# A mixture-of-experts layer split by choice: first choices placed and computed first, second choices scattered beside the first expert tiles, results in a ring of 18 tiles

## What is computed

```python
def _L0_ffn_ref(x, router_w, w1, w2, w3):
    logits = flat @ router_w.T
    topk_probs, topk_idx = jax.lax.top_k(softmax(logits), 2)
    topk_probs = topk_probs / (sum(topk_probs) + 1e-09)
    h = silu(flat @ w1[e].T) * (flat @ w3[e].T)      # for the chosen experts e; 341 wide
    out = sum over the two choices of gate * (h @ w2[e].T)
```

## Time and profile before

| what | us |
|---|---|
| median of 3 timed runs | 1537.77 (1532.89 to 1538.66) |
| the profiled execution, its own time | 1534.53 |
| its span, first to last instruction | 1532.7 |
| busy: PE / DVE / ACT / POOL | 1106.3 / 916.4 / 650.8 / 571.1 |

### The profile page before, as it was taken

The page is one execution under the profiler, slowest core; times in us unless marked ns, Lnnn a source line. Parts: engine busy times, 40 slices in busy tenths (PEclk is TensorE's granted clock), DMA queues, the critical chain, the costliest instruction groups (busy, mean ns, idle before and its releaser), DMA issues.

```text
span 1532.7 us, 23197 instructions
## 1 busy us (share of the span) xinstructions
PE 1106.3 (72%) x6172; PEld 880.5 (57%) x6172; DVE 916.4 (60%) x3422; ACT 650.8 (42%) x1813; POOL 571.1 (37%) x575
## 2 busy tenths in 40 slices
PE   3454578128784039999999946759999499999970
PEld 3444466115563028888888723335554299999970
DVE  5555578865887015555555569686763255555545
ACT  3777747203442002222222247726775144444430
POOL 2000000000677744444444400005777455555553
PEclk9999999999985569999999979968999699999995
DMA  9991000000111112222222370001121122222228
GB/s 236 428 430 83 2 1 1 0 0 1 41 53 53 52 45 60 58 62 61 59 61 60 117 246 15 0 0 36 53 67 51 47 74 70 70 72 69 70 59 308
DMA packets 60177, 125.43 MB, mean 82 GB/s; under 512 B 13148, under 2 KB 40676, under 8 KB 58512
## 3 DMA queue, kind: packets, MB, share of 16 engines
q0 software_dynamic: 20000, 73.21, 12.8%
q1 hardware_dynamic: 40048, 50.76, 11.7%
HBM read 50.75 MB, written 74.99 MB: 82 GB/s over the span
## 4 chain that ended last, share of the span: by engine, by line
PE 56%; DVE 19%; ACT 8%; issue 7%; POOL 6%; DMA 3%; SPq 1%; DVEq 0%; POOLq 0%; ACTq 0%
PE bank L1288 15%; PE bank L1279 8%; PE bank L1276 6%; PE bank L1277 6%; POOL rows L869 6%; PE bank L366 3%; PE bank L181 2%; PE bank L1465 2%; PE bank L1472 2%; PE bank L1264 2%; PE bank L1439 2%; DMA u<-planes 2%; ACT work L1379 1%; PE bank L1400 1%; ACT u L215 1%
## 5 line engine op out<-in xcount | busy, mean ns | idle before, releaser
L1150 POOL DMA_INDIRECT planes<-pay,goal x284 | 294.9, 1038 | 305.4 <-DVE pay L1197 251.0
L869 POOL DMA_INDIRECT rows<-pay,slot x256 | 251.9, 984 | 383.1 <-issue 346.7
L1288 PE MATMUL bank<-pay 128*128 128x128 f32 (+1 forms) x1988 | 275.1, 278 | 0.5 <-DVE pay L1216 0.2
L1288 PEld LDWEIGHTS bank<-pay 128*128 128x128 f32 (+1 forms) x1988 | 255.2, 191 | 26.6 <-DVE pay L1216 16.5
L1244 ACT ACTIVATE pay<-bank 128x256 f32<-128x256 f32 (+1 forms) x213 | 81.4, 382 | 309.4 <-PE bank L1277 275.3
L1248 ACT ACTIVATE pay<-bank,pay 128x256 f32<-128x256 f32 x284 | 125.8, 474 | 163.7 <-PE bank L1279 163.6
L1216 DVE TENSOR_TENSOR pay<-pay,bank 128x256 f32<-128x256 f32 (+1 forms) x213 | 82.7, 415 | 129.2 <-ACT pay L1244 128.7
L1170 DVE COPY pay<-wreg 128x1066 f32 (+1 forms) x142 | 100.0, 704 | 71.5 <-issue 66.4
L1279 PE MATMUL bank<-pay 128*128 128x256 f32 x568 | 135.9, 383 | 0.6 <-DVE pay L1180 0.6
L1276 PE MATMUL bank<-pay 128*128 128x256 f32 (+1 forms) x426 | 127.9, 382 | 0.6 <-DVE pay L1180 0.6
L1277 PE MATMUL bank<-pay 128*128 128x256 f32 (+1 forms) x426 | 127.2, 380 | 0.0
(11 more groups left out here) (387 smaller groups left out, 1984.4 us busy)
## 6 DMA issues: line engine op xcount, KB each, us to landing
rows<-pay POOLq DMA_DIRECT2D x10, 3432.0 KB, 55.6
pay<-rows SPq DMA_DIRECT2D x142, 130.0 KB
u<-planes SPq DMA_DIRECT2D x64, 256.0 KB, 5.9
planes<-pay,goal POOLq DMA_INDIRECT x284, 2.3
wreg<-in_w SPq DMA_DIRECT2D x1, 4264.0 KB, 24.9
wreg<-in_w SPq DMA_DIRECT2D x1, 4120.0 KB, 13.0
X<-in_x SPq DMA_DIRECT2D x2, 2048.0 KB, 20.1
rows<-pay,slot POOLq DMA_INDIRECT x256, 2.3
```

Of the source, the lines that this page charges most:

```text
L869: self.nc.gpsimd.indirect_dma_start(out=xs, out_offset=bass.IndirectOffsetOnAxis(ap=self.t["slot"][:, k, q:q + 1], axis=0), in_=self.t["pa ...
L1150: nc.gpsimd.indirect_dma_start(out=planes, out_offset=bass.IndirectOffsetOnAxis(ap=t["goal"][:, j * 2 + h:j * 2 + h + 1], axis=0), in_=t[" ...
L1288: ins = T.matmul(ps[4 + j % 2][:, h * P:(h + 1) * P], t["hh"][c][0:n, h * P:(h + 1) * P], t["wst"][j % 2][0:n, at + c * P:at + (c + 1) * P ...
```

## The change

It does five things, in `SPLIT = (True, False)` the first three for layer 0 alone.

1. First and second choices are ranked apart (16 running counts in place of 8), the first choices of each expert placed ahead of its second ones. `scatter` sends only the 64 columns of first choices. The row numbers of second choices need the totals, and `second_slots` makes them inside `table`.
2. `table` orders the tiles in three parts: tiles that hold first choices only ("pure"), the tiles where first choices end, and the rest. `PURE` = 25 is the least number of pure tiles that there can be (8192 first choices, 8 experts with up to 255 left over each). SP waits for all first choices before tile 0, and for all second ones before tile 25.
3. POOL sends the 64 columns of second choices between the tiles: 8 transfers, then the two that give back tile 0 (`give_back`), 8, the two of tile 1, and so on, until all 64 are sent and 8 tiles given back; from then on only results.
4. Both layers: results go into a ring of 18 tiles in `work`. DVE's wait for the transfer that last read the buffer is now on a count (`freed`) that POOL raises in `give_back(j)`, when the results of tile j-3 have landed; `finish(j)` waits for it from tile 18 on.
5. Layer 0: `finish(j-1)` and `weights(j+1)` stand ahead of the three `hh` products of tile j, as in layer 1.

The diff, cut to its core (index changes, memory layout and the wider running count are left out):

```diff
+SPLIT = (True, False)
+PURE = -(-(TOKENS - E8 * (TS - 1)) // TS)
+RING = 18
+EACH = 8
...
         own.chain(V.tensor_tensor(group(r["o2"]), group(r["b"]), per_q(c["mx"]), ALU.is_equal))
-        own.chain(V.tensor_tensor(r["o"], r["o1"], r["o2"], ALU.add))
-        own.chain(V.tensor_tensor_scan(r["i"], self.K[:, K_RESET:K_RESET + E8 * GQ], r["o"], 0.0, ALU.mult, ALU.add))
-        own.chain(V.tensor_tensor(r["e"], r["i"], r["o"], ALU.subtract))
-        V.tensor_tensor(by_expert(r["e"]), by_expert(r["e"]),
-                        self.t["carry"][:, g, :].unsqueeze(2).to_broadcast([P, E8, GQ]), ALU.add).then_inc(s("picked"), 1)
-        V.tensor_tensor(self.t["carry"][:, g + 1, :], self.t["carry"][:, g, :], by_expert(r["i"])[:, :, GQ - 1],
+        n = self.ways * E8 * GQ
+        marks, i, e = self.marks(), r["i"][:, 0:n], r["e"][:, 0:n]
+        if not self.split:
+            own.chain(V.tensor_tensor(marks, r["o1"], r["o2"], ALU.add))
+        own.chain(V.tensor_tensor_scan(i, self.K[:, K_RESET:K_RESET + n], marks, 0.0, ALU.mult, ALU.add))
+        own.chain(V.tensor_tensor(e, i, marks, ALU.subtract))
+        V.tensor_tensor(by_expert(e), by_expert(e), self.t["carry"][:, g, :].unsqueeze(2).to_broadcast(
+            [P, self.ways * E8, GQ]), ALU.add).then_inc(s("picked"), 1)
+        V.tensor_tensor(self.t["carry"][:, g + 1, :], self.t["carry"][:, g, :], by_expert(i)[:, :, GQ - 1],
                         ALU.add).then_inc(s("carried"), 1)
         dve.wait_ge(s("carried"), self.past("carried", g + 1))
+
+    def marks(self):
+
+        r = self.t["rt"]
+        return r["o"] if self.split else r["s"]
...
+        T.matmul(self.rank, self.K[:, K_TRI:K_TRI + P], self.marks(), start=True, stop=False)
+        T.matmul(self.rank, ones, r["e"][:, 0:self.ways * E8 * GQ], start=False, stop=True).then_inc(self.s("rank"), 1)
...
+        second = self.t["second"] if self.split else self.t["slot"][:, 1, :]
...
-            for k in range(2):
-                self.nc.gpsimd.indirect_dma_start(
-                    out=xs, out_offset=bass.IndirectOffsetOnAxis(ap=self.t["slot"][:, k, q:q + 1], axis=0),
-                    in_=self.t["pay"][k][:, q, :], in_offset=None, bounds_check=E8 * CAP - 1, oob_is_err=False,
-                ).then_inc(self.s("sent"), 16)
+            for k in range(1 if self.split else 2):
+                self.send(q, k, xs).then_inc(self.s("sent"), 16)
+
+    def send(self, q, k, xs):
+
+        return self.nc.gpsimd.indirect_dma_start(
+            out=xs, out_offset=bass.IndirectOffsetOnAxis(ap=self.t["slot"][:, k, q:q + 1], axis=0),
+            in_=self.t["pay"][k][:, q, :], in_offset=None, bounds_check=E8 * CAP - 1, oob_is_err=False)
+
+    def all_sent(self, eng):
+
+        eng.wait_ge(self.s("sent"), sum(SENT[:self.layer + 1]))
...
+        if self.split:
+            own.inc(V.tensor_tensor(count[:, 2 * E8:3 * E8], self.total[:, E8:2 * E8], one_base, ALU.subtract))
+            own.chain(V.tensor_tensor(count[:, E8:2 * E8], self.total[:, 0:E8], one_base, ALU.subtract))
+            own.inc(V.tensor_scalar(count[:, 0:E8], count[:, E8:2 * E8], 1.0 - TS, None, ALU.add))
+            own.chain(V.tensor_tensor(count[:, 2 * E8:3 * E8], count[:, 2 * E8:3 * E8], count[:, E8:2 * E8], ALU.add))
+        else:
+            own.chain(V.tensor_tensor(count, self.total, one_base, ALU.subtract))
+        cmp = tb["cmp"][:, 0:n * 32].rearrange("p (e i) -> p e i", i=32)
+        own.chain(V.tensor_tensor(cmp, count.unsqueeze(2).to_broadcast([P, n, 32]),
+                                  iota.unsqueeze(1).to_broadcast([P, n, 32]), ALU.is_gt))
+        own.chain(V.tensor_reduce(k, cmp, AX.X, ALU.add))
...
+        if self.split:
+            self.second_slots(own, count[:, E8:2 * E8], one_base, tb["f"][:, 0:E8], tb["look"])
         own.chain(V.memset(self.t["goal"], NOWHERE))
...
+    def second_slots(self, own, ahead, base, step, look):
+
+        V, second = self.nc.vector, self.t["second"]
+        look = look.rearrange("p (q e) -> p q e", e=E8)
+        own.inc(V.tensor_copy(step[:, 0:1], ahead[:, 0:1]))
+        own.inc(V.tensor_tensor(step[:, 1:E8], ahead[:, 1:E8], ahead[:, 0:E8 - 1], ALU.subtract))
+        own.chain(V.tensor_tensor(look, second.unsqueeze(2).to_broadcast([P, N, E8]),
+                                  base.unsqueeze(1).to_broadcast([P, N, E8]), ALU.is_ge))
+        own.chain(V.tensor_tensor(look, look, step.unsqueeze(1).to_broadcast([P, N, E8]), ALU.mult))
+        own.chain(V.tensor_reduce(self.t["after"], look, AX.X, ALU.add))
+        V.tensor_tensor(self.t["slot"][:, 1, :], second, self.t["after"], ALU.add).then_inc(self.s("second"), 1)
...
-        pool.wait_ge(S("a0_dup"), 2 * g + 2)
+        pool.wait_ge(S("a0_xh2" if route.split else "a0_dup"), 2 * g + 2)
...
+        if route.split and j == PURE:
+            sp.wait_ge(S("route_sent_second"), 16 * N * sum(SPLIT[:layer + 1]))
...
-    for j in range(NT):
+
+    def give_back(j):
+
         pool.wait_ge(s("goal"), past("goal", j + 1))
+        if j >= 3:
+            pool.wait_ge(s(f"back{j % 3}"), past(f"back{j % 3}", 32 * (j // 3)))
+            pool.nop().then_inc(s("freed"), 1)
         pool.wait_ge(s("ys"), past("ys", j + 1))
         for h in range(2):
             nc.gpsimd.indirect_dma_start(
                 out=planes, out_offset=bass.IndirectOffsetOnAxis(ap=t["goal"][:, j * 2 + h:j * 2 + h + 1], axis=0),
-                in_=t["ysb"][j % 3][:, h, :], in_offset=None, bounds_check=2 * TOKENS - 1, oob_is_err=False,
+                in_=t["ysb"][j % RING][:, h, :], in_offset=None, bounds_check=2 * TOKENS - 1, oob_is_err=False,
             ).then_inc(s(f"back{j % 3}"), 16)
-
-
-def experts_dve(nc, dve, own, S, t, ps, layer):
+    j = 0
+    if route.split:
+        pool.wait_ge(S("route_second"), sum(SPLIT[:layer + 1]))
+        pool.wait_ge(S(f"a{layer}_dup"), TILES)
+        for q in range(N):
+            route.send(q, 1, xs).then_inc(S("route_sent_second"), 16)
+            if q % EACH == EACH - 1:
+                give_back(j)
+                j += 1
+    for j in range(j, NT):
+        give_back(j)
...
-        if j >= 3:
-            dve.wait_ge(s(f"back{j % 3}"), past(f"back{j % 3}", 32 * (j // 3)))
-        V.tensor_tensor(t["ysb"][j % 3], y, gate, ALU.mult).then_inc(s("ys"), 1)
+        if j >= RING:
+            dve.wait_ge(s("freed"), past("freed", j - RING + 1))
+        V.tensor_tensor(t["ysb"][j % RING], y, gate, ALU.mult).then_inc(s("ys"), 1)
 
     if layer == 0:
         dve.wait_ge(S("w0_in"), 16)
     else:
         dve.wait_ge(S("w1_in"), 32)
         dve.wait_ge(S("b2p_in"), 32)
-    dve.wait_ge(S("route_sent"), 32 * N * (layer + 1))
+    route.all_sent(dve)
     weights(0)
     turned(0)
     for j in range(NT):
+        if j >= 1:
+            finish(j - 1)
+        if j + 1 < NT:
+            weights(j + 1)
         if layer == 0:
-            if j + 1 < NT and j == 0:
-                weights(1)
             for c, (a, w) in enumerate(CH0):
                 n = 3 * j + c
                 dve.wait_ge(s("hs"), past("hs", n + 1))
                 if j >= 1:
                     dve.wait_ge(s("down"), past("down", n - 2))
                 V.tensor_tensor(t["hh"][c][0:w, :], t["hs"][c][0:w, :], ps[c][0:w, TS:2 * TS], ALU.mult).then_inc(s("hh"), 1)
...
-                if c == 0 and j >= 1:
-                    finish(j - 1)
-                    if j + 1 < NT:
-                        weights(j + 1)
-        else:
-            if j >= 1:
-                finish(j - 1)
-            if j + 1 < NT:
...
-        t["ysb"] = [room(PAY, 2 * P).rearrange("p (h c) -> p h c", h=2) for _ in range(3)]
+        t["ysb"] = [work[:, k * TS:(k + 1) * TS].rearrange("p (h c) -> p h c", h=2) for k in range(RING)]
```

More of the change, by code:

```diff
@@ L847, in place @@
             dve.wait_ge(own.sem, n2)
-            V.tensor_reduce(self.t["slot"][:, 1, qs], group(r["b"]), AX.X, ALU.add).then_inc(s("slots"), 1)
+            V.tensor_reduce(second[:, qs], group(r["b"]), AX.X, ALU.add).then_inc(s("slots"), 1)
         dve.wait_ge(s("exp"), self.past("exp", (g + 1) * (2 - self.layer)))
@@ L877, in table @@
         tb = self.t["tb"]
-        base, iota = K[:, K_BASE:K_BASE + E8], K[:, K_IOTA:K_IOTA + 32]
+        parts = 3 if self.split else 1
+        n = parts * E8
+        count, k, end, start, u, m, e, f = (tb[name][:, 0:n] for name in ("n", "k", "end", "start", "u", "m", "e", "f"))
         j, j256 = K[:, K_J:K_J + 1], K[:, K_J256:K_J256 + 1]
-        off = K[:, K_OFF + self.layer * E8:K_OFF + (self.layer + 1) * E8]
-        dve.wait_ge(s("total"), self.past("total", 1))
-        own.chain(V.tensor_tensor(tb["n"], self.total, base, ALU.subtract))
@@ L889, in table @@
-        own.inc(V.tensor_scalar(tb["u"], tb["start"], -float(TS), j256, ALU.mult, ALU.add))
-        own.chain(V.tensor_scalar(tb["m"], tb["start"], j, None, ALU.is_le))
-        own.chain(V.scalar_tensor_tensor(out=tb["m"], in0=tb["end"], scalar=j, in1=tb["m"], op0=ALU.is_gt, op1=ALU.mult))
```

(17 more changed lines are left out.)

103 lines of the change are left out of this document (60 added, 43 removed).

## The result

The kernel after the change takes 1470.87 us (1470.02 to 1471.96), the one before 1535.99 in the same runs: a ratio of 0.9577 (0.9555 to 0.9599). The profiled execution of after took 1470.02 us with a span of 1468.2, against 1534.53 and 1532.7. The forecast's sum for it was 1472.8.

What follows compares the result with a forecast made beforehand. Tile 0 of layer 0 waits for POOL's queue of scatter issues; then PE bounds the tiles, with a hole in each. The sum 1534.5 - 55.6 - 15.9 + 9.8 = 1472.8 gave 1473 us, range 1463 to 1488.

Steps and rivals of the forecast that it cites:

- The start of the tiles: Layer 0, first transpose of tile 0: with only 64 first-choice columns sent ahead of it, it comes 55.6 us earlier.
- the wider counts' 0.3 us: Routing, layer 0: wider count matmuls and running count of the last groups add 0.3 us before the last first-choice send.
- The order on DVE: Layer 0 tiles: finish and weights ahead of the hh products close PE's hole, gaining 15.9 us, a tile of 4.18.
- 69 x 0.23: Layer 0: 69 tiles each gain PE's whole 0.23 us hole ahead of the second down chunk, 15.9 us in all.
- The pause: Layer 0, near tile 23: DVE, and PE with it, wait for POOL's give_back(7), costing 9.8 us, bounds 0 and 18.
- `finish(22)` needs `freed` at 5, which `give_back(7)` raises, and it stands at the head of tile 23: Layer 0, DVE: counted from the last first-choice send, finish(22) is due at 104.8 us, give_back(7) at 114.6, 9.8 late.
- tile 23 has already moved by more: Layer 0, tile 25: its wait for second choices, 7.2 us late, adds nothing, hidden behind tile 23's 9.8.
- The two costs: POOL's time to give_back(7), layer 0: weights copies lengthening issues, 7.7 us, and one long gap between issues, 2.84 us.
- The long gap of 2.84 us: POOL, layer 0: one 3.14 us gap ahead of the 113th send, where 0.30 is usual; expected again, lower bound 0.
- The clock: PE around the pause: its clock may drop for a moment, 0 to 1.5 us, left out of the sum.
- POOL in time: Rival on the layer 0 pause: copies cost POOL nothing, pause term 0, 1463 to 1466 us; chance 0.15.
- The rival in which sends slow the tiles down so much that nothing is won: Layer 0: send pitch of 2.24 us, not 1.29, tile 23 waits over 71 us, 1534 and above; chance 0.02.

Runs made afterwards that it cites:

- RING = 14: The changed kernel with a ring of 14 result tiles in place of 18: 1479.35 us, 0.9622 of the kernel before; on another chip 1602.48, 0.986.
- EACH = 12: The changed kernel with 12 sends between two results of POOL, not 8: 1468.10 us, 0.9554 of the kernel before; on another chip 1603.27, 0.9876.

## Why the prediction was right, and where it was not

**The start of the tiles** was forecast 55.6 us earlier and came 57.9 us earlier. The chain was the right one. The last two groups' 16 sends start in one run from 479.88 to 499.13, where 501.3 was reckoned. The gates came not the wider counts' 0.3 us later but earlier, the last of them here, for 490.00:

```profile
488.44 0.17 DVE L876 TENSOR_TENSOR pay<-rc 128x8 f32<-128x8 f32 x1
```

The first gates were 0.9 us earlier already (388.52 for 389.44), and DVE was that early ahead of any routing (its first addition to `X` of that stage stands at 356.39, where it stood at 357.34). So some 57.0 are the split's own; where the 0.9 come from isn't known. The table ended at 497.9, 3.0 us ahead of the 500.9 reckoned, and hid as said.

**The order on DVE**: forecast 15.9 us, measured 12.9 in the trace of after, 13.8 by itself and 13.1 by its removal on D. The mechanism held, cover and all: in the tile shown above DVE waits for PE ahead of `finish`, the first product is over at 705.39, 0.39 us ahead of its loads at 705.78, and the hole is closed. The size was off in the term "69 x 0.23". From the start of the group of four loads to that of the eight, after takes 0.77 us and before 1.03, which gives back 0.26; but from the eight to the next tile's first load it takes 0.96 (703.29 - 702.33), and before took 0.89 (705.92 - 705.03). The loads behind the hole had caught up 0.07 of it. So closing it is worth 0.19 a tile and the pace is 4.22, not 4.18.

**The pause** was forecast at 9.8 us and measured at 5.3, and the step that failed is "`finish(22)` needs `freed` at 5, which `give_back(7)` raises, and it stands at the head of tile 23": `freed` was put at the time at which the engine issues `give_back(7)` (114.6 after the last first choice; that issue came at 612.24, 113.1 after, so this much was right). The sequencer raises the count some 16 us ahead of that issue, as `RING = 14` shows. With that, `finish(22)`, due at 605.4, is not late, nothing else moves tile 23, and the step "tile 23 has already moved by more" falls with it: the wait for the second choices, which was to be hidden, is bare. Its own working was nearly right. The first transpose of tile 25 was reckoned at 118.9 and due at 111.7; it came at 616.30, which is 117.2, and was due at 612.44 by the pace, which is 113.3. The 7.2 us late become 3.9. So a wait at the wrong place gave a term of the right kind, and the sum is good by some luck: 4.5 us too much of pause and 2.3 too little gain at the start stand against 3.0 too much gain from the order and 1.0 of small terms left out.

**The two costs** counted into POOL's time: the copies were put at 7.7 us and cost 8.8 (7.4 of it in the sends, the rest in results), by the cause named, as the copies on ScalarE show. The long gap of 2.84 us didn't come in layer 0, where the 113th issue is now one of a mixed series. It is in the trace of before in both layers; why it comes was not tried.

**The clock** was left out at 0 to 1.5 us; it costs 1.4 in tile 25. The measured 5.3 of the pause hold that, where the forecast's 9.8 were waiting alone. Tile 0 of layer 0 takes 7.04 us where it took 6.35, and that is the clock as well: the windows of just this tile show a granted clock of 0.60 where before had 0.67. After 9.5 us of idleness (68 before) PE did the pairs of L1352 and L1353 at 1.2 GHz, 0.85 us apart, up to 510.2, 4.3 us from the first one; before did so up to 566.4 only, 2.7 us from the first. At 0.43 us a pair those 1.6 us are worth about 0.8. Layer 1 was put at zero, and from tile 70 on there are 0.3 us.

With the measured terms: 1534.5 - 57.9 - 12.9 + 5.3 + 0.7 + 0.3 = 1470.0, the profiled execution's 1470.02. The rival "POOL in time", 1463 to 1466, had as its outcome what the trace of `EACH = 12` shows, no pause (1464.40 in its profiled execution, 1468.10 in the median); its reason, copies that cost nothing, was wrong. The rival in which sends slow the tiles down so much that nothing is won fell on A and B. On C and D its outcome is partly true, though not its way, since tile 23 doesn't wait for POOL: some 40 of the 65 us are gone on D, by waits for which the trace has no releaser in the program.

## What to carry to other kernels

Where one queue both feeds a stage and drains it, write down the due time of each thing behind it, and look for the last of one kind: here the pause hung on the last send, and fewer results ahead of it (`EACH = 12`) took it away. A count that POOL raised by a `nop` came when its sequencer passed it, not when the engine did; if a count is to say that earlier transfers are done, let it be raised by one of them. Before a scatter is split, look at what makes the second part's row numbers, and when: in layer 1 that was the limit. A copy on DVE beside indirect issues costs what is left of it when the next issue starts. And run such a kernel on more than one chip before its gain is quoted: 65 us here were 25 there.

## What was not expected of the hardware

- POOL's sequencer runs ahead of its engine: 17.2 us in layer 0 of after, 11.2 us in layer 1, and before had it too, in the source view of its scatter (last MOVE of layer 0 at 545.7, last issue at 556.9).
- A DVE copy of 0.72 us lengthens the indirect issue that starts 0.21 us into it from 0.98 to 1.36 us, one that starts 0.45 into it to 1.12: the rest of the copy, less 0.13. Most issues that began ahead of a copy took no harm.
- After 3.7 us in which PE did nothing, busy up to them, it ran at 1.2 GHz (granted clock 0.50 from 616.30 to 618.30), and the eight passes took 1.92 us for 1.13.
- How long PE stays at 1.2 GHz when it starts again differs between two starts alike: 2.7 us from the first product of tile 0 before, 4.3 after.
- The kernel before takes 1536 to 1537 us on two chips and 1625 to 1628 on two others. In the changed kernel on D the loss that the change adds stands as idle time of ACT, DVE and PE beside a POOL that issues 20 to 30 times in a row, up to 14.5 us at a time; beside pairs of issues it is absent.
